# Folding a layer norm's gamma and beta into the next weight, and a new order of work, in a graph transformer on one NeuronCore

## The chip, the cores and the metric

The kernel is written in Bass, with every wait and signal placed by hand, and runs on one core of one Trainium2 chip. The metric is the device time of one execution in microseconds, as a median of several runs. The engines are TensorE (PE; PEld is its weight load), VectorE (DVE), ScalarE (ACT), GpSimd (POOL) and SyncE (SP), which issues all loads and stores from one queue. Each engine works through its own instructions in order; they meet only at semaphores.

## The reference, cut to what matters

Eight graphs of 1024 nodes with 256 features each. `h = relu(layernorm(x))` goes through three layers of the first network, the result is added to `x`, and the same is done with one attention layer (`_L1_gnn_ref`) whose output passes an ELU.

```python
for l in range(3):                                   # first network
    si = x @ attn_w[l, :d]
    sj = x @ attn_w[l, d:]
    scores = si[:, :, None] + sj[:, None, :] + attn_b[l]
    scores = jnp.where(scores >= 0, scores, 0.2 * scores)
    scores = jnp.where(mask, scores, -jnp.inf)
    attn = jax.nn.softmax(scores, axis=-1)
    agg = jnp.einsum('bij,bjd->bid', attn, x)
    h = layernorm(x + agg, g1[l], beta1[l])
    ff = jax.nn.gelu(h @ W1[l] + b1[l], approximate=False) @ W2[l] + b2[l]
    x = layernorm(h + ff, g2[l], beta2[l])
```

The attention layer is the same without bias and FFN: `Wh = h @ W`, scores from `Wh`, softmax over the neighbours, `elu(attention @ Wh)`. A row without neighbours gets the mean over all nodes.

## The kernel before

The 32 pairs of graph and layer are 32 steps in a hand-written `ORDER`: 24 FFN steps (layers 0 to 2) and 8 attention steps (layer 3; k = 6, 10, 14, 18, 22, 29, 30, 31), neighbours in the list belonging to different graphs. A graph's nodes are NT = 8 tiles of 128.

A step k first aggregates: `aggregate(k, t)` multiplies the unnormalised scores `pw` (f32, 1024 x 1024) by the node rows `xx`, 16 instructions for each tile t, into one of two PSUM banks OB. In an FFN step VectorE divides by the row sum, adds the residual into `xc` and takes statistics (`residual1`), GpSimd makes the reciprocal deviation (`ln_rstd`), ScalarE normalises, GpSimd multiplies by gamma and adds beta (`affine`, lines 541 and 543), TensorE transposes pairs of tiles into TH (`transpose_h`), and ScalarE and VectorE write the transposed rows as an f16 high half and an f16 low half (`hT`). Then come 16 passes n over the hidden features: `hidden(k, n)` makes 512 columns of the first product into bank FB (6 instructions), ScalarE does the GELU and writes its high half, VectorE (even n, line 1100) or GpSimd (odd n, line 554) the low half into `gT`, a ring of three, and `second(k, n)` adds the second product into OB (12 instructions). `hidden` runs LAG = 2 passes ahead. The bias b2 is the first product of each bank: `ones3` times `b2r`, four times a step. `residual2`, the second statistics and `affine` with the second gamma and beta end the step; GpSimd does the last four tiles of that (`tail`) at the head of the next step.

Between these pieces each step prepares the scores of step q = k + 1. VectorE sums the two score columns (`scores`, lines 1003 and 1008), splits them (`columns`), TensorE transposes them into TP (`transpose_c`, line 1498) and spreads them over RB (`spread_s1`, `spread_sj`), VectorE takes each row's masked maximum (`row_max`, line 1063), ScalarE writes the shifted mask `nms` (line 780), and then come 16 units: TensorE transposes half a tile row of the mask into one half of RB (`unit`), VectorE makes the scores from it (`score`, line 1086) and ScalarE exponentiates (line 765). A unit waits until the score two units earlier has left its half of RB. When each piece is due stands in tables by place: 0 to 7 are the aggregation tiles, 8 + n the passes, END the end of the step, -1 the place before tile 0. Which table a step uses depends on its `variant`: "early", "late", "very late", and "ahead" (q = 11, 15, 19, 23), where columns and maxima are already made two steps earlier.

In an attention step the aggregated rows go through `elu_a` and `elu_b` on VectorE and `final` on GpSimd. Eight steps (`GAT_AT`) also make the input of an attention step: x is loaded again (`x1_of`), added, normalised, transposed (line 1538), multiplied by the weight (`gat_product`) and summed (`gat_colsum`). Seven steps (`RAW_AT`) also load and normalise a new graph and convert its edges (line 1111).

The first layer's weights are split into f16 high and low halves at the start (`w0_low`), the others in steps 0 and 1 (`load_piece`, `piece_high`, `piece_low`), stored to DRAM, and loaded back at each change of layer.

TensorE's order in an FFN step before:

```python
for t in range(NT):
    aggregate(k, t)
    if t in (4, 6):
        transpose_h(k, t // 2 - 2)
    prepare(k, t)
...
for n in range(LAG):
    hidden(k, n)
...
transpose_h(k, 2)
```

## Time and profile before

| | |
|---|---|
| median of 3 runs | 2702.7 us (2700.8 to 2707.65) |
| profiled execution | 2699.2 us, span from first to last instruction 2697.5 us |
| TensorE busy | 2357.2 us, 87% |
| VectorE, ScalarE, GpSimd busy | 1833.0, 1566.6, 1286.5 us |
| mean granted TensorE clock | 0.957 |
| DMA | 128 MB, 48 GB/s over the span |

Spans are read against the profiled execution, which lies 3.5 us under the median. The steps are cut at the first aggregation product of each: step 0 begins at 57.4 us, step 2 at 247.9, step 5 at 504.6, step 10 at 968.7, step 14 at 1290.9, step 26 at 2270.0, step 29 at 2531.0, step 31 at 2662.7.

### The profile page before, as it was taken

The numbers are of one execution on the slowest core, as the hardware profiler recorded it, in microseconds if no ns is written. First come the engines' busy times: TensorE is split into PE (matmuls) and PEld (weight loads), VectorE is DVE, ScalarE is ACT, GpSimd is POOL, SyncE is SP. The second block draws the span as 40 slices with busy tenths as digits, with TensorE's granted clock in tenths as the row PEclk, the third lists the DMA queues.
The fourth block names the chain that finished last, engine by engine and source line by source line (L and its number), as shares of the span: only waits on it lengthen the run. The fifth ranks groups of instructions, "written<-read, shape, count | busy, mean of one in ns | idle before, by whom it ended". The sixth has DMA issues, their size and how long they took to land.

```text
span 2697.5 us, 41567 instructions
## 1 busy us (share of the span) xinstructions
PE 2357.2 (87%) x14721; PEld 1760.6 (65%) x14721; DVE 1833.0 (68%) x4906; ACT 1566.6 (58%) x2423; POOL 1286.5 (48%) x2212
## 2 busy tenths in 40 slices
PE   3889999878899989899798988999888999999868
PEld 2566666646676666676576766677665677667656
DVE  7677677437677667776677766868657576666655
ACT  4457666445566555565556665665636556656544
POOL 5555465523365434644356542655434555446411
PEclk9999999989899999999899998999989999999988
DMA  4312021101120112110211102111121010100000
GB/s 175 123 40 86 5 86 40 52 4 40 59 87 5 40 43 91 52 36 9 73 61 55 36 13 74 56 52 36 38 92 40 24 36 9 36 9 21 23 12 30
DMA packets 66051, 128.15 MB, mean 48 GB/s; under 512 B 12956, under 2 KB 53172, under 8 KB 62772
## 3 DMA queue, kind: packets, MB, share of 16 engines
q1 hardware_dynamic: 65844, 125.50, 14.0%
q8 instruction: 116, 1.90, 0.3%
q14 instruction: 91, 0.75, 0.1%
HBM read 110.80 MB, written 14.68 MB: 47 GB/s over the span
## 4 chain that ended last, share of the span: by engine, by line
PE 57%; DVE 21%; ACT 8%; POOL 6%; issue 6%; DMA 1%; SPq 0%; DVEq 0%; POOLq 0%; ACTq 0%
PE OB L1413 35%; PE FB L1413 13%; DVE mj L1063 5%; PE RB L1413 4%; DVE pw L1086 4%; ACT nms L780 3%; DVE junk L1003 2%; PE TH L1413 2%; DMA adjst<-in_x 1%; DVE st L952 1%; DVE junk L1008 1%; POOL xc L541 1%; DVE xc L979 1%; ACT xc L725 1%; ACT gT L759 1%
## 5 line engine op out<-in xcount | busy, mean ns | idle before, releaser
L1413 PE MATMUL OB<-xx,pw 128*128 128x257 f32 x4096 | 980.4, 398 | 26.0 <-DVE xc L979 16.7
L1413 PEld LDWEIGHTS OB<-xx,pw 128*128 128x128 f32 x4096 | 798.3, 199 | 168.7 <-DVE xc L979 21.1
L1413 PE MATMUL FB<-hT,wb 128*128 128x512 f16 x2304 | 564.1, 383 | 67.6 <-DVE gT L1100 42.0
L1413 PE MATMUL OB<-wb,gT 128*128 128x256 f16 x4608 | 575.2, 273 | 4.3 <-POOL gT L554 4.2
L1413 PEld LDWEIGHTS OB<-wb,gT 128*128 128x128 f16 x4608 | 449.8, 98 | 137.5 <-POOL gT L554 8.1
L554 POOL TENSOR_TENSOR gT<-g,gT 128x512 f16<-128x512 f32 x192 | 229.2, 1194 | 612.7 <-ACT gT L759 612.3
L725 ACT ACTIVATE xc<-xc,nb,rs 128x256 f32<-128x256 f32 x384 | 212.8, 589 | 375.3 <-POOL nb L529 375.2
L1086 DVE SCALAR_TENSOR_TENSOR pw<-r2s,sj,RB 128x512 f32<-128x512 f32 x512 | 365.4, 740 | 77.6 <-PE RB L1413 74.7
L1413 PEld LDWEIGHTS FB<-hT,wb 128*128 128x128 f16 x2304 | 212.9, 98 | 276.7 <-DVE gT L1100 49.1
L541 POOL TENSOR_TENSOR xc<-xc,gb 128x256 f32<-128x256 f32 x384 | 289.9, 755 | 94.0 <-ACT xc L725 94.0
L765 ACT ACTIVATE pw<-pw,sj 128x512 f32<-128x512 f32 x512 | 327.7, 708 | 8.6 <-DVE pw L1086 8.3
L1063 DVE CUSTOM_DVE_ANT_0 mj<-RB,nm 128x1024 bf16<-128x1024 f32 x256 | 303.3, 1215 | 3.7 <-issue 2.9
L1413 PE MATMUL RB<-identb,nms 128*128 128x128 bf16 x2048 | 207.2, 236 | 106.8 <-DVE pw L1086 82.5
L780 ACT ACTIVATE nms<-nm,cc 128x1024 bf16<-128x1024 bf16 x256 | 279.7, 1136 | 8.9 <-DVE cc L1078 8.9
L1100 DVE TENSOR_TENSOR gT<-FB,gT 128x512 f16<-128x512 f32 x192 | 132.2, 688 | 216.2 <-ACT gT L759 216.0
L1413 PEld LDWEIGHTS RB<-identb,nms 128*128 128x128 bf16 x2048 | 149.3, 104 | 154.8 <-DVE pw L1086 118.3
L754 ACT ACTIVATE FB<-FB,b1c 128x512 f32<-128x512 f32 x192 | 125.8, 655 | 163.2 <-PE FB L1413 162.9
L521 POOL TENSOR_SCALAR ve<-mv 128x2 f32<-128x2 f32 x256 | 58.2, 227 | 321.8 <-DVE mv L955 307.4
L962 DVE RECIPROCAL rden<-OB 128x1 f32<-128x1 f32 x192 | 31.8, 166 | 246.4 <-PE OB L1413 245.9
L754 ACT ACTIVATE g<-FB,b1c 128x512 f32<-128x512 f32 x192 | 130.9, 682 | 114.1 <-PE FB L1413 114.1
L526 POOL TENSOR_TENSOR rs<-ve,mhalf 128x2 f32<-128x2 f32 x256 | 180.0, 703 | 21.3
L1008 DVE CUSTOM_DVE_ANT_0 junk<-xx,aw 128x256 bf16<-128x256 f32 x256 | 165.4, 646 | 0.0
(112 smaller groups left out, 2565.6 us busy)
## 6 DMA issues: line engine op xcount, KB each, us to landing
wb<-w_scratch SPq DMA_DIRECT2D x19, 2048.0 KB, 7.8
adjst<-in_adj SPq DMA_DIRECT2D x56, 512.0 KB, 4.2
xx<-in_x SPq DMA_DIRECT2D x16, 512.0 KB, 5.5
nm<-in_L_gnn_W SPq DMA_DIRECT2D x6, 1024.0 KB, 9.4
gb<-in_L_gnn_g SPq DMA_DIRECT2D x48, 128.0 KB, 2.8
gb<-in_L_gnn_beta SPq DMA_DIRECT2D x48, 128.0 KB, 3.4
adjst<-in_x SPq DMA_DIRECT2D x6, 1024.0 KB, 6.8
out_x<-adjst SPq DMA_DIRECT2D x48, 128.0 KB, 1.7
```

Of the source, the lines that this page charges most:

```text
L526: pool.tensor_tensor(out=rs[:, kind, c], in0=ve[:, kind, c], in1=mhalf[:, :], op=ALU.pow)\
L541: pool.tensor_tensor(out=v, in0=v, in1=gb[:, 0, :], op=ALU.mult).then_inc(mul_done[kind], 1)
L554: pool.tensor_tensor(out=gT[:, i % GRING, 1, :], in0=g32[:, :], in1=gT[:, i % GRING, 0, :], op=ALU.subtract).then_inc(glo_odd, 1)
L725: act.activation(dst, src, ACT.Relu if kind in (LNR, LNG) else ACT.Identity, bias=nb[:, kind, t:t + 1], scale=rs[:, kind, t:t + 1])\
L754: act.activation(dst, src, ACT.Gelu, bias=b1c[:, layer(k), f:f + 1], scale=1.0 / W_SCALE)\
L765: act.activation(v, v, ACT.Exp, bias=sj2[:, q % 2, jt:jt + 1]).then_inc(exp_done, 1)
L780: act.activation(nms[:, it, :], nm[:, slot(q), it, :], ACT.Identity, bias=cc[:, it:it + 1])\
L1008: dve.tensor_tensor_reduce(out=junk[:, 1, :], in0=src, in1=aw[:, l, 1, :], scale=1.0, scalar=0.0, op0=ALU.mult, op1=ALU.add, accum_out=sc[ ...
L1063: dve.tensor_tensor_reduce(out=mj[:, n % 2, :], in0=RB[:, :], in1=nm[:, g % 3, t, :], scale=1.0, scalar=-3e38, op0=ALU.add, op1=ALU.max, a ...
L1086: dve.scalar_tensor_tensor(out=pw[:, jt, half], in0=r2s[:, half], scalar=sj8[:, q % 2, jt:jt + 1], in1=RB[:, (u % 2) * HALF:(u % 2 + 1) * ...
L1100: dve.tensor_tensor(out=gT[:, i % GRING, 1, :], in0=FB[i % 2][:, :], in1=gT[:, i % GRING, 0, :], op=ALU.subtract).then_inc(glo_even, 1)
L1413: return pe.matmul(o, lhsT, rhs, start=first, stop=last)
```

## The change

**Fold.** The first gamma multiplies the rows of W1 when it is split (`g1s`, times the scale of 64), and W1 times beta is added to b1 (`bias_product`, 16 one-column products for each layer, and `bias_sum`). The transposes then read rows that are only normalised. The residual still needs gamma and beta: GpSimd's `affine` waits for the transpose of its pair, and stands in the passes n = 1, 3, 9 and 11. It adds beta plus b2, a sum made once, stored in `bb_scratch` and loaded in beta's place; the four `ones3` products of each FFN step are gone.

**Order on TensorE.** `hidden(k, 0)` and `hidden(k, 1)` stand ahead of the last aggregation tile; the transposes follow tiles 3, 5 and 7 and pass 2.

**Preparation.** `transpose_c` moves behind tile 0, the spreads to tiles 1 to 3, and the maxima are spaced further apart. For the steps in `CARRY` (0, 1, 6, 7, 11, 15, 19, 23, 24, 30, 31) the last four units are left to that step's own tiles 0 and 1 (step 6: the last eight, tiles 0 to 2), and some units use TH and TP in place of RB. In attention steps a unit is scored and exponentiated in its own tile. Score sums ahead of steps 12, 16, 20 and 24 move into the attention steps' tiles 0 to 3. In step 5 the work for the attention input moves from the aggregation into the passes.

**Loads.** At the start the first layer's score weights come first; the rows of b1, g1 and beta1 come ahead of most of the edges; the other score weights come last. In a step the load of x for the attention input is issued before gamma and beta of the second normalisation. The selector `sel` is built from 8 columns and copied out by VectorE.

```diff
-MAX_FE = {2: (0,), 3: (1,), 4: (2,), 5: (3,), 6: (4, 5), 7: (6, 7)}
+CARRY = {0} | {k for k in range(1, STEPS) if is_gat(k - 1) or k in VERY_LATE}
+GAT_FFN_LATE = {5}
...
+MAX_FE = {2: (0,), 3: (1,), 4: (2,), 5: (3,), 6: (4,), 7: (5,), 8: (6,), 9: (7,)}
...
+MAX_FD = {3: (0, 1), 4: (2,), 5: (3, 4), 6: (5,), 7: (6, 7)}
...
+UNITS_FE = {11: (0, 1), 12: (2,), 13: (3,), 14: (4, 5), 15: (6,), 16: (7,), 17: (8,), 18: (9, 10), 19: (11,),
+            20: (12,), 21: (13, 14), 22: (15,)}
...
+UNITS_FC = {11: (0, 1), 12: (2, 3), 13: (4, 5), 14: (6, 7), 15: (8, 9), 16: (10, 11), 17: (12, 13, 14, 15)}
...
+        if k in CARRY:
+            return dict(col=None, ct=0, s1=1, sj=3, row=MAX_FD, units=UNITS_FE, shift=SHIFT_FE)
...
-            return dict(col=None, ct=-1, s1=0, sj=1, row=MAX_FE, units=UNITS_FC, shift=SHIFT_FC)
-        return dict(col=None, ct=-1, s1=0, sj=1, row=MAX_FE, units=UNITS_FE, shift=SHIFT_FE)
+            return dict(col=None, ct=0, s1=1, sj=2, row=MAX_FC, units=UNITS_FC, shift=SHIFT_FC)
+        return dict(col=None, ct=0, s1=1, sj=2, row=MAX_FE, units=UNITS_FE, shift=SHIFT_FE)
...
+def carried(k):
+
+    if k not in CARRY:
+        return {}
+    if k - 1 in GAT_FFN_LATE:
+        return {0: (8, 9, 10, 11), 1: (12, 13), 2: (14, 15)}
+    return {0: (12, 13), 1: (14, 15)}
+
+
+def score_bank(q, u):
+
+    if q in CARRY and u in (8, 9, 12, 13, 14, 15):
+        return ("TH", "TP")[u % 2]
+    return ("R0", "R1")[u % 2]
...
-                load_gb(gb1, g1, beta1, 0, gb1_ready)
                 load_gb(gb2, g2, beta2, 0, gb2_ready)
+                sp.wait_ge(bb_done, 1)
+                sp.dma_start(bb_scratch.rearrange("l d -> (l d)").unsqueeze(0), st1[0:1, 0:LAYERS * D])\
+                    .then_inc(bb_stored, 16)
+                sp.wait_ge(bb_stored, 16)
+                load_gb(gb1, g1, bb_scratch, 0, gb1_ready)
...
-                if l < LAYERS and k > 0:
-
-                    sp.wait_ge(aff_done[1], 8 * fi(k))
-                    load_gb(gb2, g2, beta2, l, gb2_ready)
                 if k in GAT_AT:
                     gg = GAT_AT[k]
                     if gg < 6:
...
                     sp.dma_start(x1_of(gg), x_v[gg]).then_inc(x1_ready, 16)
+                if l < LAYERS and k > 0:
+
+                    sp.wait_ge(aff_done[1], 8 * fi(k))
+                    load_gb(gb2, g2, beta2, l, gb2_ready)
...
                 for r in [32 * v + NT * part for v in range(2) for part in range(3)]:
-                    pool.affine_select(out=sel[:, :, :], in_=sel[:, :, :], compare_op=ALU.not_equal,
-                                       fill=1.0, base=-r, pattern=[[-1, NT], [0, P]],
+                    pool.wait_ge(const_ready, n)
+                    pool.affine_select(out=sel8[:, :], in_=sel8[:, :], compare_op=ALU.not_equal,
+                                       fill=1.0, base=-r, pattern=[[-1, NT]],
                                        channel_multiplier=1).then_inc(const_ready, 1)
...
-                pool.wait_ge(norm_done[kind], n)
+                if kind == LN1:
+                    pool.wait_ge(ht_done, 4 * fi(k) + t // 2 + 1)
+                else:
+                    pool.wait_ge(norm_done[kind], n)
...
+                    if n == 11:
+                        ln_rstd(LN2, i, 0)
+                    if n in (1, 3, 9, 11):
+                        j = (1, 3, 9, 11).index(n)
+                        affine(LN1, k, 2 * j)
+                        affine(LN1, k, 2 * j + 1)
...
+            act.wait_ge(g1s_done, 1)
+            act.wait_ge(w0_ready, 32)
+            for kd in range(KD):
+                c = slice(kd * FF, (kd + 1) * FF)
+                act.activation(wb[:, 0, c], nm2.bitcast(f32)[:, c], ACT.Identity, bias=zero1[:, 0:1],
+                               scale=g1s[:, 0, kd:kd + 1]).then_inc(w0_hi, 1)
+            act.activation(wb[:, 2, :], nm2.bitcast(f32)[:, 2048:4096], ACT.Copy, scale=W_SCALE).then_inc(w0_hi, 1)
...
             def gat_step(k):
                 gat = GAT_AT.get(k)
-                before(k)
                 for t in range(NT):
                     elu_a(k, t)
                     if t >= 1:
                         elu_b(k, t - 1)
                     prepare(k, t)
-                    unit_scores(k, t)
+                    for u in carried(k).get(t, ()):
+                        score(k, u)
+                    for u in prep_tables(k)["units"].get(t, ()):
+                        score(k + 1, u)
...
+            def bias_sum(l):
+
+                dve.wait_ge(bw_done, l + 1)
+                dve.tensor_tensor(out=b1c[:, l, :], in0=TPf[:, 0:FT], in1=b1c[:, l, :], op=ALU.add)\
+                   .then_inc(b1c_done, 1)

...
+            def bias_product(l):
+
+                if l == 0:
+                    pe.wait_ge(w0_ready, 32)
+                    pe.wait_ge(wc_done, 1)
+                else:
+                    pe.wait_ge(piece_ready, 16 * (2 * l - 1))
+                pe.wait_ge(*tp_after[-1])
+                raw = nm2[:, 0:4096].bitcast(f32)
+                for f in range(FT):
+                    for kd in range(KD):
+                        ins = mm(TPf[:, f:f + 1], raw[:, kd * FF + f * P:kd * FF + (f + 1) * P],
+                                 be1[:, l, kd:kd + 1], kd == 0, kd == KD - 1)
+                ins.then_inc(bw_done, 1)
+                tp_after.append((b1c_done, l + 1))
...
                     if f == 0:
                         u = bank_uses(k) + NT + 2 * h + b
                         pe.wait_ge(ob_free, u - 1)
-                        mm(OB[b][:, :].rearrange("p (c d) -> p c d", c=2), ones3[:, :],
-                           b2r[:, layer(k):layer(k) + 1, :].broadcast_to([P, 2, D]), True, False)
                     if b == 0:
                         pe.wait_ge(*glo(i))
                     w2h, w2l = wb[:, 2, f * D:(f + 1) * D], wb[:, 3, f * D:(f + 1) * D]
...
-                    pe.wait_ge(x_done, 16 * q + u - 1)
+                if b == "TH" and th_after:
+                    pe.wait_ge(*th_after[-1])
+                elif b == "TP":
+                    pe.wait_ge(*tp_after[-1])
+                elif u >= 2:
+                    pe.wait_ge(x_done, 16 * q + (u - 3 if q in CARRY and u in (10, 11) else u - 1))
                 for i in range(HT):
-                    c = (u % 2) * HALF + i * P
-                    ins = mm(RB[:, c:c + P], nms[:, HT * h + i, jt * P:(jt + 1) * P], identb[:, :], True, True)
+                    ins = mm(BANK[b][:, i * P:(i + 1) * P], nms[:, HT * h + i, jt * P:(jt + 1) * P],
+                             identb[:, :], True, True)
                 ins.then_inc(mt_done, 1)
+                if b == "TH":
+                    th_after.append((x_done, 16 * q + u + 1))
+                elif b == "TP":
+                    tp_after.append((x_done, 16 * q + u + 1))
...
                 gat = GAT_AT.get(k)
-                early = k + 1 not in VERY_LATE
-                prepare(k, -1)
+                early = gat is not None and k not in GAT_FFN_LATE
                 for t in range(NT):
+                    if t == NT - 1:
+                        hidden(k, 0)
+                        hidden(k, 1)
                     aggregate(k, t)
-                    if t in (4, 6):
-                        transpose_h(k, t // 2 - 2)
                     prepare(k, t)
-                    if gat is not None and not early:
...
+                    if t in (3, 5, 7):
+                        transpose_h(k, t // 2 - 1)
                 for n in range(NF):
                     prepare(k, 8 + n)
...
+                    if k in GAT_FFN_LATE:
+                        if n in (1, 2, 4, 5):
+                            gat_product(gat, (1, 2, 4, 5).index(n))
+                        if n in (0, 1, 2, 4):
+                            gat_transpose(gat, (0, 1, 2, 4).index(n))
+                    if n == (3 if k in GAT_FFN_LATE else 2):
                         transpose_h(k, 3)
```

## Rows read from the trace of the kernel before

**Rows 1.** The page, part 1: busy us (share of the span) xinstructions.

```profile
PE 2357.2 (87%) x14721; PEld 1760.6 (65%) x14721; DVE 1833.0 (68%) x4906; ACT 1566.6 (58%) x2423; POOL 1286.5 (48%) x2212
```

**Rows 2.** The view of the cores: span, mean granted clock.

```profile
core 0: 2697.5 us, clock 0.957
```

**Rows 3.** TensorE's groups by shape: busy us, mean ns | idle before, releasers.

```profile
L1413 PE MATMUL OB<-xx,pw 128*128 128x257 f32 x4096 | 980.4, 398 | 26.0 <-DVE xc L979 16.7 <-DVE hT L1156 9.3
...
L1413 PE MATMUL FB<-hT,wb 128*128 128x512 f16 x2304 | 564.1, 383 | 67.6 <-DVE gT L1100 42.0 <-issue 21.1 <-DVE hT L1094 4.4
L1413 PE MATMUL RB<-identb,nms 128*128 128x128 bf16 x2048 | 207.2, 236 | 106.8 <-DVE pw L1086 82.5 <-ACT nms L780 11.6 <-DVE M L1063 10.5
L1437 PE MATMUL TH<-ident,xc 128*128 128x128 f32 x384 | 59.2, 277 | 22.3 <-POOL xc L543 21.5 <-ACT xx L790 0.8
L1413 PE MATMUL TH<-gw,mj 128*128 128x256 f16 x384 | 51.8, 289 | 28.7 <-DVE mj L1136 20.1 <-DVE hT L1094 8.6
```

**Rows 4.** The view of waits: us in total, times, longest.

```profile
PE TP L1498 <- DVE c L1031: 47.5, 16, 29.2
```

**Rows 5.** Windows: start, k=0, 2, 5, 14; length, busy by engine, clock, DMA.

```profile
core 0: us, PE busy (x) PEld busy (x) DVE busy (x) ACT busy (x) POOL busy (x), PEclk, DMA share, GB/s
0.00:57.40 57.40, 11.87 (x82) 7.49 (x83) 43.63 (x104) 25.14 (x31) 33.96 (x60) 1.00 0.57 204
57.40:163.70 106.30, 86.87 (x521) 62.66 (x518) 76.37 (x184) 60.16 (x90) 55.30 (x90) 0.93 0.28 92
247.90:331.50 83.60, 79.56 (x518) 58.13 (x518) 55.48 (x147) 52.69 (x80) 43.67 (x73) 1.00 0.10 32
504.60:642.50 137.90, 100.70 (x599) 72.42 (x599) 69.29 (x201) 66.38 (x105) 56.54 (x106) 0.88 0.13 43
1290.90:1347.00 56.10, 43.35 (x194) 33.55 (x194) 35.40 (x105) 29.52 (x49) 14.73 (x24) 0.80 0.19 68
```

**Rows 6.** Windows of k=10, 14, 18, 22 alone: their sum and mean.

```profile
sum 208.20, PE 163.57 PEld 127.60 DVE 140.50 ACT 117.79 POOL 58.94; mean PE 40.89 PEld 31.90 DVE 35.12 ACT 29.45 POOL 14.74
```

**Rows 7.** Timeline of TensorE in k=2: start us, us, what.

```profile
286.88 0.38 PE L1413 MATMUL OB<-b2r,ones 128*128 128x512 bf16 x1
287.10 0.82 PE L1413 MATMUL OB<-wb,gT 128*128 128x256 f16 x6
...
294.81 1.46 PE L1413 MATMUL FB<-hT,wb 128*128 128x512 f16 x6
...
297.41 0.61 PE L1413 MATMUL RB<-identb,nms 128*128 128x128 bf16 x8
```

**Rows 8.** The groups of instructions: GpSimd's low half and its multiplication by gamma.

```profile
L541 POOL TENSOR_TENSOR xc<-xc,gb 128x256 f32<-128x256 f32 x384 | 289.9, 755 | 94.0 <-ACT xc L725 94.0
L554 POOL TENSOR_TENSOR gT<-g,gT 128x512 f16<-128x512 f32 x192 | 229.2, 1194 | 612.7 <-ACT gT L759 612.3
```

**Rows 9.** Timeline of ScalarE in k=26: in brackets the idle time before.

```profile
2284.70 1.09 ACT L725 ACTIVATE xc<-xc,nb,rs 128x256 f32<-128x256 f32 x2 [3.73 <-POOL nb L529]
```

**Rows 10.** Timeline of VectorE in k=10.

```profile
971.43 0.42 DVE L1008 CUSTOM_DVE_ANT_0 junk<-xx,aw 128x256 bf16<-128x256 f32 x1
...
972.47 1.22 DVE L1063 CUSTOM_DVE_ANT_0 mj<-RB,nm 128x1024 bf16<-128x1024 f32 x1
...
984.03 0.94 DVE L1008 CUSTOM_DVE_ANT_0 junk<-xx,aw 128x256 bf16<-128x256 f32 x1
...
995.82 1.40 DVE L1086 SCALAR_TENSOR_TENSOR pw<-r2s,sj,RB 128x512 f32<-128x512 f32 x2
```

**Rows 11.** Timeline of TensorE in k=10.

```profile
996.62 1.26 PE L1413 MATMUL RB<-identb,nms 128*128 128x128 bf16 x8 [3.31 <-DVE pw L1086]
```

**Rows 12.** The chain of waits in k=5: start us, us, what.

```profile
518.44 7.39 DMA adjst<-in_x
```

**Rows 13.** Timeline of TensorE in k=29.

```profile
2570.90 1.11 PE L1538 MATMUL TP<-ident,mj 128*128 128x128 f32 x4 [12.30 <-ACT mj L725]
```

**Rows 14.** Timeline of all engines at the start.

```profile
14.79 7.82 POOL L505 TENSOR_SCALAR_AFFINE_SELECT sel<-sel 64x1024 bf16<-64x1024 bf16 x6
...
28.92 2.95 DVE L1111 TENSOR_SCALAR nm<-pw 128x1024 bf16<-128x1024 int32 x4
```

529 lines of the change are left out of this document (271 added, 258 removed).

## The prediction

> **What bounds the kernel now.** The page comes first: TensorE is busy for 2357.2 us of the 2697.5 us span, VectorE for 1833.0, ScalarE for 1566.6, GpSimd for 1286.5 [rows 1]. So TensorE sets the time, and 340 us of its span are idle. The view of the cores adds a second loss: the mean granted clock is 0.957 [rows 2], and 4.3% of 2697.5 us is 116 us of clock not granted (where that falls into idle time it costs nothing).
>
> TensorE's groups by shape say what the idle time waits for [rows 3]: the mask products into RB waited 106.8 us, 82.5 of it for VectorE's score instruction at L1086; the first FFN product into FB 67.6 us, mostly for the low half of gT at L1100; the transposes of the normalised rows 22.3 us, 21.5 for GpSimd's affine at L543; the attention products into TH 28.7 us; the aggregation 26.0. The view of waits adds the c transposes, 47.5 us, of which the longest, 29.2, is the start [rows 4].
>
> The windows, cut where each step's aggregation begins, say where [rows 5]. An ordinary FFN step (k=2) takes 83.6 us with 79.6 busy. The exceptions are the start (57.4 us, 11.9 busy), k=0 (106.3, 86.9) and k=5 (137.9, 100.7, clock 0.88). The four attention steps k=10, 14, 18 and 22, each ahead of a step whose preparation was begun two steps early, take 208.2 us with 163.6 busy [rows 6]; k=14 runs at a clock of 0.80 [rows 5]. In all there are 24 FFN steps and 8 attention steps.
>
> **The change, part by part.**
>
> *Bias products removed.* Each FFN step issues four b2r products, and the next instruction follows one after 0.22 us (286.88 to 287.10) [rows 7]. 96 x 0.22 = 21 us on the engine that sets the time. They wait for VectorE to empty a bank; the first real product inherits that wait, so I count nothing for it. Bounds: 19 (some passes wait for another engine anyway) and 24 (at the half clock). Gain 21.
>
> *Transposes no longer wait for gamma and beta.* GpSimd does two instructions per tile, L541's at 0.755 us [rows 8] and another of the same shape, so a pair of tiles puts 3.0 us between normalisation and transpose. But the transposes also move one tile earlier (behind tiles 3 and 5 rather than 4 and 6), which takes a tile of about 3.5 us of cover away. At k=26, which begins at 2270.0, ScalarE starts the first pair at 2284.70, released by GpSimd, which is still in the tail of the step before when the first statistics come [rows 9]; it ends 15.8 us into the step, and the fourth tile ends at 14 to 15 us. So in ordinary steps this edit breaks even, and in k=0 and 23, where the next graph's statistics stand ahead of it, a stall stays. Gain 10 of 22.3, bounds 0 and 20.
>
> *Two FFN products before the last aggregation tile.* The GELU, its copy and the subtraction for products 0 and 1 now run under that tile, and the third product, which waits for them, finds them done. FB's 67.6 us are 2.8 a step. A little comes back, since the last pair's normalisation must fit in before product 4. Gain 42, bounds 20 and 60. If the cover is gone, because the second transposes come late, the stall stands ahead of product 0 and the gain is 20.
>
> *The affine moves into the FFN loop* (n = 1, 3, 9, 11). A pass is 2.6 us of TensorE (294.81 to 297.41) [rows 7], and GpSimd's subtraction, 1.19 us [rows 8], comes every second pass, so 5.2 us hold 1.19 + 3.0 = 4.2 us. In the eleven steps that also carry a next graph's or an attention input's work it is more: k=5 has 56.5 us of GpSimd against 43.7 in k=2 [rows 5], 12.9 in four portions of 3.2, and 4.2 + 3.2 is 7.4 in 5.2: 2.2 us late, of which half is hidden by the ring of three. Cost 10, bounds 0 and 40.
>
> *Mask products and scores.* Sixteen score instructions close a step's preparation; VectorE does two in 1.40 us [rows 10]. Four of the sixteen now go into the next step's first tiles in eleven steps, and TH and TP are two more banks between the engines. In attention steps a unit is scored in its own tile instead of one tile later; that is the 3.31 us wait at 996.62 and shorter ones behind it [rows 11], and of the 11 us idle in such a step I take 7. VectorE gets two tiles' score sums (four of 0.42 us, 1.7 in all) in each of those steps' first four tiles, beside its own work under 3.5 us: about level. Of the 96 us of RB waits behind the start: gain 50, bounds 20 and 75. The aggregation's 26.0 us are mostly waits at the head of attention steps behind VectorE's queue, which is shorter by two tiles of score sums and a mask row of 1.22 us [rows 10]: gain 12, bounds 0 and 20.
>
> *The c transpose* moves from before tile 0 to behind it. Of the 18.3 us inside steps: gain 12, bounds 5 and 16. The mask rows that follow later have passes of TensorE to hide under.
>
> *k=5, k=29 and the order of loads.* At k=5 GpSimd sat behind the load of x (7.39 us at 518.44) [rows 12] with the first pair's statistics queued behind it. That load is now issued before gamma and beta of the second normalisation, and the attention products go into the FFN loop. At k=29 a transpose held TensorE for 12.30 us [rows 13] with ready aggregation tiles queued behind it; it now stands one tile later. Of 28.7 + 12.3 us: gain 24, bounds 10 and 35. New is the end of k=5, where eight mask rows of 1.22 us [rows 10], 9.8 in all, fall in four passes of 2.6: cost 6, bounds 0 and 12.
>
> *The start.* The selector's six instructions took 7.82 us of GpSimd and now work on 8 columns; VectorE's four mask conversions, 2.95 us [rows 14], leave the place between the c transpose and its copy; and four of sixteen units leave the start at 0.7 us each. 2.6 + 2.8 less 0.4 for the new bias products: gain 5, bounds 0 and 8.
>
> *The clock.* Low clocks stand where the idle time is: 0.88 in k=5 and 0.80 in k=14 against 1.00 in k=2 [rows 5]. With half the idle time gone a bit less than half of the 116 us should return. Gain 50, bounds 20 and 90.
>
> Sum: 21 + 10 + 42 - 10 + 50 + 12 + 12 + 24 - 6 + 5 + 50 = 210 us. Laid over the steps that is: the four attention steps 58 (208 to 150), k=5 31 (138 to 107), k=0 and 23 together 22, the last attention steps and k=6 20, the start 5, and 3.5 in each of the 21 other FFN steps. Against the profiled execution's own 2699.2 us it makes 2489; the median of the runs shown is 3.5 us higher, so 2492.
>
> One row speaks against moving the affine: a score sum at L1008 takes 0.42 us in one place and 0.94 in another, where GpSimd is busy [rows 10]. The Trainium skill, "SBUF — State Buffer", section "Who interferes with whom", says that VectorE and GpSimd share one port pair as an exclusive lock, which VectorE instructions with both inputs in SBUF also take; by that rule, the trace agrees. Its consequence here is the second rival, priced from rows.
>
> **The rivals.**
>
> *VectorE stays in the way (18%).* Its work is moved, not less. If its queue in attention steps and at the end of k=5 sets the pace, the scores give 20, the clock 25, the aggregation 4, the attention terms 14: 73 less, 2565. For it: VectorE is busy 35 of the 52 us of such a step [rows 6]. Against: it has waits in their last tiles.
>
> *VectorE and GpSimd slow each other (8%).* In eleven steps four score sums fall beside the moved affines, each 0.52 us longer, and what follows waits: 11 x 2.1 = 23 us, 2515.
>
> *More falls away than I count (17%).* With TensorE fed all through, the clock gives 90 and the scores 65: 2437.
>
> *GpSimd becomes the bound, slower than before (4%).* If the four affine pairs stand wholly ahead of a subtraction that a product waits for, 24 x 4 x 3.0 = 288 us are added: 2780. It ends slower once some 73% of them is exposed. Against: GpSimd is busy 43.7 of 83.6 us in k=2 [rows 5], and the residual wants the affine only at n = 8.
>
> *Only the removed products count (3%):* every stall just moves, 2682.
>
> **How the numbers follow.** My forecast, 2492 us, has 50%, with a range of its own of 2460 to 2530. The range for 8 in 10 takes in the second rival, the third and most of the first: 2435 to 2580. A difference under 0.3% (8 us) can't be told from none. Faster by more has 0.95, the same 0.01, slower 0.04.
>
> **What would show it.** No b2r products; FB's waits under 30 us; the transposes waiting for ScalarE, not GpSimd; RB's waits under 60 us; the four attention steps at 36 to 40 us with a clock above 0.93; ordinary FFN steps at 80 to 81 us; k=5 near 107. It is wrong if products wait for gT of L554 for more than 30 us, if attention steps stay above 45 us, or if the mean clock stays at 0.96.

## The result, and the profile after

The changed kernel takes 2634.65 us (median of 4 runs, 2623.89 to 2639.5) against 2701.75 us before (4 runs, 2700.29 to 2707.65), a ratio of 0.9742 with a 95% interval of 0.9709 to 0.9776. The forecast was 2492, its range 2435 to 2580. The kernel is faster, as forecast, but by 67 us and not by 210. The profiled execution took 2635.33 us.

Part 1 of the page and the view of the cores, against [rows 1, 2]:

```profile
PE 2320.5 (88%) x14721; PEld 1733.9 (66%) x14721; DVE 1848.1 (70%) x4914; ACT 1579.8 (60%) x2426; POOL 1271.1 (48%) x2199
```

```profile
core 0: 2633.6 us, clock 0.973
```

TensorE is busy for 37 us less and idle for 313 us, where 340 were idle before; the granted clock rose from 0.957 to 0.973. TensorE's groups by shape, against [rows 3]:

```profile
L1484 PE MATMUL OB<-xx,pw 128*128 128x257 f32 x4096 | 960.0, 389 | 22.2 <-DVE xc L1025 13.1 <-DVE hT L1203 8.5 <-ACT pw L799 0.4
L1484 PE MATMUL OB<-wb,gT 128*128 128x256 f16 x4608 | 574.1, 275 | 27.6 <-DVE xc L1025 18.1 <-POOL gT L612 9.5
L1484 PE MATMUL FB<-hT,wb 128*128 128x512 f16 x2304 | 568.5, 385 | 73.9 <-DVE gT L1147 57.3 <-issue 11.4 <-ACT g L788 5.2
L1484 PE MATMUL RB<-identb,nms 128*128 128x128 bf16 x1784 | 164.9, 227 | 83.5 <-DVE pw L1133 65.3 <-ACT nms L816 14.2 <-DVE M L1109 3.5
L1525 PE MATMUL TH<-ident,xc 128*128 128x128 f32 x384 | 59.9, 280 | 24.3 <-ACT xc L757 24.3
L1484 PE MATMUL TH<-gw,mj 128*128 128x256 f16 x384 | 48.7, 278 | 19.6 <-DVE mj L1183 18.5 <-DVE hT L1141 1.2
```

FB's waits were to fall from 67.6 us to under 30 and are 73.9. RB's were to fall from 106.8 to under 60 and are 83.5. The transposes wait for ScalarE now, but as long as before. The c transpose's line in the view of waits was 47.5 us in 16 waits [rows 4]; now it is:

```profile
PE TP L1584 <- DVE c L1077: 11.8, 2, 11.1
```

Of these 11.8 us, 11.1 are the start. A wait of another kind is new: in k=30 a c transpose waits 3.5 us for a unit's score to leave TP.

The windows of the start, k=0, 2, 5 and 10, cut as in [rows 5], and the sum of the four attention steps alone, against [rows 6]:

```profile
core 0: us, PE busy (x) PEld busy (x) DVE busy (x) ACT busy (x) POOL busy (x), PEclk, DMA share, GB/s
0.00:44.70 44.70, 15.78 (x99) 13.39 (x99) 34.89 (x103) 21.68 (x25) 18.54 (x47) 1.00 0.75 271
44.70:159.50 114.80, 93.05 (x548) 68.17 (x546) 75.58 (x175) 58.80 (x88) 48.89 (x80) 0.88 0.25 85
254.80:336.80 82.00, 77.52 (x513) 58.09 (x513) 54.87 (x147) 50.82 (x77) 43.37 (x73) 1.00 0.09 33
510.30:620.00 109.70, 92.38 (x561) 67.17 (x562) 64.99 (x191) 59.15 (x96) 56.86 (x106) 0.92 0.16 54
948.10:982.60 34.50, 31.77 (x176) 26.64 (x177) 31.34 (x100) 29.46 (x49) 14.42 (x24) 1.00 0.21 80
```

```profile
sum 138.00, PE 127.07 PEld 106.54 DVE 125.38 ACT 117.83 POOL 57.71; mean PE 31.77 PEld 26.64 DVE 31.34 ACT 29.46 POOL 14.43
```

Cut by steps in this way, each step from its first aggregation product to the next one's, the two profiled executions are 63.9 us apart, and they divide like this (the last column is worked out from the same cut of a run told below):

| steps | before | changed | gain | predicted | three edits (E5) |
|---|---|---|---|---|---|
| start | 57.4 | 44.7 | 12.7 | 5 | 44.9 |
| attention, k=10, 14, 18, 22 | 208.1 | 138.0 | 70.1 | 58 | 138.0 |
| k=5 | 137.9 | 109.7 | 28.2 | 31 | 107.1 |
| k=6, 29, 30, 31 | 221.2 | 210.5 | 10.7 | 20 | 212.6 |
| k=0 and 23 | 205.8 | 218.9 | -13.1 | 22 | 203.4 |
| the 21 other FFN steps | 1867.0 | 1911.8 | -44.8 | 74 | 1849.7 |

The sum predicted is 210 us, the sum that came 63.9. The first four rows gave 122 us where 114 were forecast. All of the miss lies in the 23 FFN steps of the last two rows: 96 us predicted, 58 lost, a difference of 154. In the 21 ordinary ones TensorE's idle time rose from 110 to 160 us: FB's from 59 to 64, RB's from 13 to 46, OB's behind the second product from 9 (with the bias products) to 22, the attention products' from 1 to 9; of the larger groups only the c transpose's fell, from 18 to 1. By steps, 22.9 of the 44.8 us lie in k=7, 11, 15 and 19, which also prepare a new graph, 11.0 in k=1 and 10.1 in k=9, 13, 17 and 21; k=2, 4, 25, 26 and 27 are 0.9 to 1.5 us shorter each.

The timeline of k=26, which begins at 2209.7, shows the first of the causes, at the end of the aggregation (the number in brackets is the idle time of the engine before):

```profile
2240.08 0.60 ACT L793 ACTIVATE gT<-FB 128x512 f16<-128x512 f32 x1
2240.48 3.64 PE L1484 MATMUL OB<-xx,pw 128*128 128x257 f32 x16
...
2244.15 0.17 DVE L1008 RECIPROCAL rden<-OB 128x1 f32<-128x1 f32 x1 [3.04 <-PE OB L1484]
...
2245.43 0.66 DVE L1147 TENSOR_TENSOR gT<-FB,gT 128x512 f16<-128x512 f32 x1
...
2246.15 1.47 PE L1484 MATMUL FB<-hT,wb 128*128 128x512 f16 x6 [1.60 <-DVE gT L1147]
...
2246.92 0.20 POOL L584 TENSOR_TENSOR nb<-ng,rs 128x2 f32<-128x2 f32 x1
2247.07 1.16 POOL L612 TENSOR_TENSOR gT<-g,gT 128x512 f16<-128x512 f32 x1
2247.15 1.09 ACT L757 ACTIVATE xc<-xc,nb,rs 128x256 f32<-128x256 f32 x2 [1.96 <-POOL nb L584]
...
2248.14 0.64 ACT L788 ACTIVATE FB<-FB,wc 128x512 f32<-128x512 f32 x1
```

The GELU of product 0 is through, with its copy, at 2240.68, under the last aggregation tile, as the prediction wanted. But its low half on VectorE starts at 2245.43: it stands behind the residual of tile 7, and VectorE sits idle for 3.04 us until that tile is summed. GpSimd's low half of product 1 stands behind the reciprocal deviation of tile 7's pair (nb, 2246.92), and ScalarE's gelu of product 2 behind that pair's normalisation (2247.15). Three in-order queues hold the chain until tile 7 is done, and the two products now ahead of that tile push it back by 2.5 us: it ends 34.4 us into the step, and 31.9 in the run below that has them behind it (E4).

The timeline of k=11, which begins at 982.6, shows the second cause:

```profile
1022.24 1.15 POOL L612 TENSOR_TENSOR gT<-g,gT 128x512 f16<-128x512 f32 x1
...
1022.63 2.45 DVE L1158 TENSOR_SCALAR nm<-adjst 128x1024 bf16<-128x1024 int32 x2
...
1023.35 1.17 POOL L599 TENSOR_TENSOR xc<-xc,gb 128x256 f32<-128x256 f32 x1
...
1024.60 1.05 POOL L601 TENSOR_TENSOR xc<-xc,gb 128x256 f32<-128x256 f32 x1
...
1026.42 0.73 POOL L601 TENSOR_TENSOR xc<-xc,gb 128x256 f32<-128x256 f32 x1
...
1027.69 0.69 DVE L1158 TENSOR_SCALAR nm<-adjst 128x1024 bf16<-128x1024 int32 x1 [0.48 <-DMA adjst<-in_adj]
1027.78 1.17 POOL L581 TENSOR_TENSOR rs<-ve,mhalf 128x2 f32<-128x2 f32 x1
...
1029.25 1.09 ACT L757 ACTIVATE xx<-xx,nb,rs 128x256 f32<-128x256 f32 x2 [2.60 <-POOL nb L584]
1029.42 0.69 DVE L1158 TENSOR_SCALAR nm<-adjst 128x1024 bf16<-128x1024 int32 x1 [1.03 <-DMA adjst<-in_adj]
...
1030.25 0.67 ACT L788 ACTIVATE g<-FB,wc 128x512 f32<-128x512 f32 x1
...
1030.97 1.04 PE L1484 MATMUL FB<-hT,wb 128*128 128x512 f16 x4 [0.78 <-ACT g L788]
```

The moved affine pair (four instructions, 1023.35 to 1027.15) stands ahead of the next graph's reciprocal deviation, whose nb releases ScalarE only at 1029.25; ScalarE had sat idle for 2.60 us with the gelu of product 3 queued behind, and TensorE waits for that gelu. The prediction had GpSimd late at its own subtraction; it is late at four small instructions for which ScalarE waits.

A third difference stands in k=0 and k=1, and the prediction's sum has nothing for it: there the new bias products (16 of them for a layer, 32 instructions in the trace) hold TensorE for 5.3 and 4.9 us (from 119.88 and from 218.46 on).

### The profile page after: what moved, and what is told of

It reads as the page before. It is cut to its first block, busy times and chain, and to the rows that moved or that the text cites. A ratio compares the mean times of both kernels' runs of the same rounds, so it can differ in the third digit from the quotient of the medians.

```text
span 2633.6 us, 41679 instructions
## 1 busy us (share of the span) xinstructions
PE 2320.5 (88%) x14721; PEld 1733.9 (66%) x14721; DVE 1848.1 (70%) x4914; ACT 1579.8 (60%) x2426; POOL 1271.1 (48%) x2199
## 3 DMA queue, kind: packets, MB, share of 16 engines
q8 instruction: 117, 1.92, 0.3%
## 4 chain that ended last, share of the span: by engine, by line
PE 55%; DVE 24%; issue 8%; ACT 8%; POOL 6%; DMA 1%; DVEq 0%; SPq 0%; POOLq 0%; ACTq 0%
PE OB L1484 36%; PE FB L1484 12%; DVE pw L1133 5%; DVE mj L1109 3%; PE RB L1484 3%; ACT nms L816 3%; DVE junk L1049 3%; DVE st L998 2%; PE TH L1484 2%; DVE gT L1147 2%; DVE xc L1025 1%; DVE junk L1054 1%; ACT gT L793 1%; POOL rs L581 1%; PE TH L1525 1%
## 5 line engine op out<-in xcount | busy, mean ns | idle before, releaser
L1484 PE MATMUL OB<-xx,pw 128*128 128x257 f32 x4096 | 960.0, 389 | 22.2 <-DVE xc L1025 13.1
L1484 PEld LDWEIGHTS OB<-xx,pw 128*128 128x128 f32 x4096 | 771.4, 193 | 163.4 <-DVE xc L1025 19.6
L1484 PE MATMUL FB<-hT,wb 128*128 128x512 f16 x2304 | 568.5, 385 | 73.9 <-DVE gT L1147 57.3
L799 ACT ACTIVATE pw<-pw,sj 128x512 f32<-128x512 f32 x512 | 334.0, 711 | 57.5 <-DVE pw L1133 57.0
L757 ACT ACTIVATE xc<-xc,nb,rs 128x256 f32<-128x256 f32 x384 | 212.6, 590 | 234.0 <-POOL nb L584 233.9
L1133 DVE SCALAR_TENSOR_TENSOR pw<-r2s,sj,RB 128x512 f32<-128x512 f32 x446 | 315.7, 738 | 43.7 <-PE RB L1484 43.0
L1484 PE MATMUL RB<-identb,nms 128*128 128x128 bf16 x1784 | 164.9, 227 | 83.5 <-DVE pw L1133 65.3
L788 ACT ACTIVATE FB<-FB,wc 128x512 f32<-128x512 f32 x192 | 125.7, 655 | 162.9 <-PE FB L1484 162.6
L1008 DVE RECIPROCAL rden<-OB 128x1 f32<-128x1 f32 x192 | 31.9, 166 | 256.0 <-PE OB L1484 255.4
L788 ACT ACTIVATE g<-FB,wc 128x512 f32<-128x512 f32 x192 | 130.7, 681 | 125.9 <-PE FB L1484 125.8
L1484 PEld LDWEIGHTS RB<-identb,nms 128*128 128x128 bf16 x1784 | 124.2, 101 | 115.3 <-DVE pw L1133 88.8
## 6 DMA issues: line engine op xcount, KB each, us to landing
adjst<-in_x SPq DMA_DIRECT2D x6, 1024.0 KB, 11.1
```

Of the source, the lines that this page charges most:

```text
L757: act.activation(dst, src, ACT.Relu if kind in (LNR, LNG) else ACT.Identity, bias=nb[:, kind, t:t + 1], scale=rs[:, kind, t:t + 1])\
L788: act.activation(dst, src, ACT.Gelu, bias=b1c[:, layer(k), f:f + 1], scale=1.0 / W_SCALE)\
L799: act.activation(v, v, ACT.Exp, bias=sj2[:, q % 2, jt:jt + 1]).then_inc(exp_done, 1)
L1133: dve.scalar_tensor_tensor(out=pw[:, jt, half], in0=r2s[:, half], scalar=sj8[:, q % 2, jt:jt + 1], in1=b, op0=ALU.max, op1=ALU.add).then_i ...
L1484: return pe.matmul(o, lhsT, rhs, start=first, stop=last)
```

## The experiments

Every run is compared with the kernel before on the same chip. "By the steps" means by the same cut of the profiled execution as in the table above. Where a difference to the changed kernel or between two runs is given, it is that of the two ratios times 2702 us; the ratios are each known to some 0.0015 to 0.003, so such a difference is good to 5 to 10 us, and where it is smaller the steps of the profiled executions carry the reading.

**E1, VectorE's first low half ahead of the last residual.**

```diff
                     if t == 7:
                         prepare(k, 7)
+                        if k not in GAT_FFN_LATE:
+                            g_low(k, 0)
                     residual1(k, t)
...
-                    if n % 2 == 0:
+                    if n % 2 == 0 and (n > 0 or k in GAT_FFN_LATE):
                         g_low(k, n)
```

> The changed kernel, in which VectorE makes the low half of the first gelu output (gT, L1147) ahead of the last residual of the aggregation instead of behind it (not in k=5). Theory A, the low half is late because it stands in VectorE's order behind a residual that waits for aggregation tile 7, while the 67 us of FB waits were predicted to fall to 30 and rose to 74: the wait of 1.60 us in front of hidden product 2 is gone in some 23 steps, FB waits fall from 74 to about 40 us, the time by 30 to 38 us to about 2600 (ratio to the kernel before 0.960 to 0.964). Rival, the wait only moves to the next consumer of VectorE's work (the low half of hT, the mask rows, the OB banks): FB falls but RB, OB or hT waits rise by as much, and the time stays within 8 us of 2634 (ratio 0.972 to 0.977).

Measured 2645.2 us, ratio 0.9775 (0.976 to 0.9789): not faster at all. FB's waits fall from 73.9 to 62.8 us and the time does not follow. In k=26, which begins at 2221.0 here, the wait of 1.60 us is gone, and one of 2.17 stands where one of 1.31 stood, a pair of passes later:

```profile
2257.43 0.69 POOL L581 TENSOR_TENSOR rs<-ve,mhalf 128x2 f32<-128x2 f32 x1
...
2258.20 0.20 POOL L584 TENSOR_TENSOR nb<-ng,rs 128x2 f32<-128x2 f32 x1
...
2258.35 1.16 POOL L612 TENSOR_TENSOR gT<-g,gT 128x512 f16<-128x512 f32 x1
...
2259.43 0.64 ACT L788 ACTIVATE FB<-FB,wc 128x512 f32<-128x512 f32 x1
...
2262.07 1.22 DVE L1109 CUSTOM_DVE_ANT_0 mj<-RB,nm 128x1024 bf16<-128x1024 f32 x1
...
2263.21 0.68 DVE L1147 TENSOR_TENSOR gT<-FB,gT 128x512 f16<-128x512 f32 x1
...
2263.95 1.47 PE L1486 MATMUL FB<-hT,wb 128*128 128x512 f16 x6 [2.17 <-DVE gT L1147]
```

The 21 ordinary steps take 1911.7 us, to a tenth what they took; k=0 and 23 take 10 us more. Theory A, VectorE's order alone, falls. GpSimd and ScalarE hold the same chain behind the same tile: product 2 is through at 2257.13, and its GELU starts at 2259.43, behind tile 7's normalisation. Its low half is then late once more, on VectorE, where mask rows, the last at 2262.07, stand ahead of it.

**E4, the two products behind the last tile again.**

```diff
                 for t in range(NT):
-                    if t == NT - 1:
-                        hidden(k, 0)
-                        hidden(k, 1)
                     aggregate(k, t)
...
+                hidden(k, 0)
+                hidden(k, 1)
                 for n in range(NF):
```

> The changed kernel with the first two hidden products behind aggregation tile 7 again, all else as changed. The prediction counted 42 us for having them ahead. Theory A, in-order VectorE takes nearly all of this back since its low half still follows the last residual: the time rises by under 12 us (ratio to the kernel before 0.973 to 0.979). Rival, the 42 us were gained and something else lost them: the time rises by 30 to 50 us (ratio 0.985 to 0.993).

Measured 2616.43 us, ratio 0.967 (0.9655 to 0.9684): 19 us faster than with the products ahead. Neither theory had this. By the steps, the 21 ordinary ones fall by 22.0 us and k=5 by 2.5, and k=0 and 23 rise by 3.9. FB's group in this run:

```profile
L1484 PE MATMUL FB<-hT,wb 128*128 128x512 f16 x2304 | 569.7, 386 | 46.0 <-DVE gT L1147 40.0 <-ACT g L788 5.1
```

Against the changed kernel's 73.9 us, the 11.4 of "issue" are gone (product 0, waiting 0.5 to 1.05 us ahead of tile 7 in steps such as k=11 at 1013.06, after VectorE made the low half of hT at 1012.27), and 17 of the wait for low halves: products 0 and 1 stand between tile 7 and product 2 again, as cover. The prediction's gain of 42 us is a loss of about 19.

**E9 and E11, nothing of the gelu chain behind tile 7** (not in k=5; the transposes of pair 3 move one pass later with it). E9 keeps the products ahead; E11 has them behind. Both have the edits of E2 and E3, below. The first hunk, VectorE's, is in E9 alone.

```diff
+                        if k not in (0, 5, 23):
+                            g_low(k, 0)
                     residual1(k, t)
...
-                ln_rstd(LN1, i, 3)
+                if k in GAT_FFN_LATE:
+                    ln_rstd(LN1, i, 3)
...
                     if n % 2 == 1:
                         g_low(k, n)
+                    if n == 1 and k not in GAT_FFN_LATE:
+                        ln_rstd(LN1, i, 3)
...
                     if n == 1:
                         ht_high(k, 2)
+                    if n == (1 if k in GAT_FFN_LATE else 2):
                         normalise_pair(LN1, k, 3)
```

> The changed kernel (first two hidden products ahead of aggregation tile 7), in which nothing of the gelu chain stands behind tile 7's statistics any more: VectorE's first low half ahead of the last residual, GpSimd's reciprocal deviation of LN1 pair 3 behind its low half of product 1, ScalarE's normalisation of that pair behind gelu 2 and TensorE's transposes of it one pass later; with the two edits that do not touch this (reciprocal deviations first at n=1 and 3; the transposes of k=0 and k=23 later, no product ahead there). Without the un-anchoring these would stand near 2588. Theory of the anchor, each of the three in-order engines holds the chain until tile 7 is summed, and a product ahead only pushes tile 7 back: now the products ahead pay, FB waits on VectorE's low halves fall to 20 to 30 us and the time to 2545 to 2568 (ratio 0.941 to 0.949), at or under the same kernel with the products behind. Rival, it is TensorE's cover that is missing (two products fewer between tile 7 and hidden product 2) whatever the order elsewhere: above 2575 (ratio over 0.952).

> The kernel of three edits (products behind tile 7) with the same un-anchoring of GpSimd, ScalarE and TensorE, without VectorE's, which has its first low half behind the last residual anyhow. Theory of the anchor: with the products behind tile 7, its statistics are there by the time that product 1 is through gelu, so the order hardly matters: within 8 us of the kernel of three edits (ratio 0.942 to 0.948). Rival, the waits of 0.8 and 1.1 us in front of hidden products 2 and 4 come from the normalisation that ScalarE makes ahead of gelu 2: they go, 10 to 30 us less (ratio 0.934 to 0.941).

E9 measured 2561.17 us, ratio 0.9489 (0.9469 to 0.9509), E11 2562.57 us, ratio 0.9486 (0.9472 to 0.9501). The 2588 that E9 is held against was reckoned (E3 less E2's part), not run, but the ordinary steps have a run to be held against: they take 1875.3 us in E3 and 1849.0 in E9, 26 less. So freeing the chain is worth 26 us with the products ahead, and the anchor is real. The waits for VectorE's low halves fell less than expected, from 57.3 in the changed kernel to 39.2 us. With the products behind, freeing the chain is worth nothing (E11 is 10 us above E5, below, and 5.7 by the ordinary steps, about the 8 that were allowed for). The freed kernel with products ahead is no better than the kernels with products behind (1849.0 us in the ordinary steps, 1849.7 in E5), so in none of these runs did they pay: with all three queues freed, they break even.

**E3, the reciprocal deviations ahead of the moved affine.**

```diff
+                    first = early and n in (1, 3)
+                    if first and raw is not None:
+                        ln_rstd(LNR, raw, n // 2)
+                    if first and gat is not None:
+                        ln_rstd(LNG, gat, n // 2)
                     if n in (1, 3, 9, 11):
...
                         affine(LN1, k, 2 * j)
...
-                        if n in (1, 3, 5, 7):
+                        if n in (5, 7):
                             ln_rstd(LNR, raw, n // 2)
...
-                    if gat is not None and early and n in (1, 3, 5, 7):
+                    if gat is not None and early and n in (5, 7):
                         ln_rstd(LNG, gat, n // 2)
```

> The changed kernel, in which GpSimd makes the reciprocal deviations of the raw or graph-attention tiles at n=1 and n=3 ahead of the two LN1 affine pairs that the change moved there, instead of behind them (13 steps that are early and have such tiles). Theory B, the moved affine pairs (two times about 4 us) hold ScalarE's normalisation and the gelu behind it: the ScalarE waits of 2.1 to 2.6 us at these places, and the FB, OB and RB waits behind them, go; 2 to 3 us in each of 11 to 13 steps, 20 to 35 us in all, to about 2607 (ratio 0.961 to 0.968). Rival, these waits are covered by TensorE's products in hand and only their tail counts: under 8 us (ratio 0.972 to 0.976).

Measured 2598.01 us, ratio 0.9599 (0.9583 to 0.9616): 39 us faster than the changed kernel, a little more than expected, for the order of eight small instructions in each of 11 steps (not 13: k=0 and 23 are not "early"). Ten of the 11 are 2.8 to 4.5 us shorter; k=3 is not. In k=11 ScalarE goes from one to the next without a wait:

```profile
1013.62 1.92 DVE L1163 TENSOR_SCALAR nm<-adjst 128x1024 bf16<-128x1024 int32 x2
...
1014.48 0.51 POOL L576 TENSOR_SCALAR ve<-mv 128x2 f32<-128x2 f32 x1
...
1016.45 0.20 POOL L584 TENSOR_TENSOR nb<-ng,rs 128x2 f32<-128x2 f32 x1
...
1017.55 1.08 ACT L762 ACTIVATE xx<-xx,nb,rs 128x256 f32<-128x256 f32 x2
...
1018.53 0.67 ACT L793 ACTIVATE g<-FB,wc 128x512 f32<-128x512 f32 x1
```

The 21 ordinary steps fall from 1911.8 to 1875.3 us, RB's waits in them from 46 to 31 (that VectorE's scores were late because the low halves were is my reading, and was not run alone).

**E12, half of the first affine left out.** The multiplication by gamma on GpSimd is gone; the residual lacks it, the FFN products do not.

```diff
-                pool.tensor_tensor(out=v, in0=v, in1=gb[:, 0, :], op=ALU.mult).then_inc(mul_done[kind], 1)
-                pool.wait_ge(mul_done[kind], n)
+                if kind != LN1:
+                    pool.tensor_tensor(out=v, in0=v, in1=gb[:, 0, :], op=ALU.mult).then_inc(mul_done[kind], 1)
+                    pool.wait_ge(mul_done[kind], n)
```

> The changed kernel with the multiplication by gamma left out of the first normalisation's affine on GpSimd (the products see the normalised values as before; the residual stream lacks gamma, so the output is another), which takes 184 instructions of 0.72 to 1.17 us off GpSimd, half of the moved work. If the moved affine's length on GpSimd is what costs, as the reordering that won 37 us says: 15 to 30 us less (ratio 0.963 to 0.969). Rival, only the order counts and not the length: under 8 us (ratio 0.971 to 0.976).

Measured 2596.41 us, ratio 0.9611 (0.9594 to 0.9627), 35 us faster, above what either theory said (the left-out instructions are 192, not 184). Half of the length buys about as much as the right order: taking it out gives 35 us, where the prediction had 10 for the cost of all of it, with a bound of 40. Not all of the 35 need be GpSimd's queue. With these instructions gone VectorE's score sums take 303.7 us in place of 315.7, so some of it may be VectorE working undisturbed, and this run does not part the two. What the same cut would give in the kernel before was not run.

**E2, the transposes of k=0 and k=23 later.**

```diff
-                    if t == NT - 1:
+                    if t == NT - 1 and k not in (0, 23):
                         hidden(k, 0)
                         hidden(k, 1)
...
-                    if t in (3, 5, 7):
-                        transpose_h(k, t // 2 - 1)
+                    if k in (0, 23):
+                        if t in (4, 6):
+                            transpose_h(k, t // 2 - 2)
+                    elif t in (3, 5, 7):
+                        transpose_h(k, t // 2 - 1)
...
+                if k in (0, 23):
+                    hidden(k, 0)
+                    hidden(k, 1)
+                    transpose_h(k, 2)
```

> The changed kernel, in which the first three transpose pairs of steps k=0 and k=23 stand behind tiles 4, 6 and 7 of the aggregation, as in the kernel before, with the first two hidden products behind tile 7; the other steps as changed. Theory C, in these two steps GpSimd takes the raw statistics of tile 2j ahead of the LN1 pair j-1, so a transpose one tile earlier holds back the aggregation tile that its own successor needs: TH waits in the two steps fall from 12.7 and 11.1 us to under 4 each, and the time by 12 to 20 us to about 2618 (ratio 0.966 to 0.970). Rival, the chain through LN1 pairs is there at any place of the transposes (it is VectorE's edges of the same stretch that makes it long): the waits move to the FB and nms products, and the time stays within 5 us (ratio 0.973 to 0.976).

Measured 2624.43 us, ratio 0.9698 (0.9682 to 0.9714), 12 us faster. The two steps fall from 218.9 to 203.2 us and no other step moves by more than 2. The edit moves the first two products as well, but E4 moved these alone, and the two steps rose to 222.8; so the place of the transposes is worth 20 us there. The transposes' waits fall only in part, from 23.8 to 14.4 us in the two steps, where under 8 were expected. With the transpose one tile earlier, aggregation tile 2j stands behind it, the next graph's statistics of pair j behind tile 2j, and the LN1 pair j-1 behind these: theory C holds, at the low end of its price, and the chain that is left is the rival's part.

**E14 and E13, the tables of the mask work as before.** In 14 FFN steps from k=7 on, and in k=4, which uses the same tables, the passes in which mask rows, shifted masks and mask products are made; E14 on the changed kernel, E13 on E5, below.

```diff
-MAX_FE = {2: (0,), 3: (1,), 4: (2,), 5: (3,), 6: (4,), 7: (5,), 8: (6,), 9: (7,)}
+MAX_FE = {2: (0,), 3: (1,), 4: (2,), 5: (3,), 6: (4, 5), 7: (6, 7)}
...
-UNITS_FC = {11: (0, 1), 12: (2, 3), 13: (4, 5), 14: (6, 7), 15: (8, 9), 16: (10, 11), 17: (12, 13, 14, 15)}
+UNITS_FC = {9 + i: (2 * i, 2 * i + 1) for i in range(8)}
```

(MAX_FC, UNITS_FE, SHIFT_FE and SHIFT_FC are put back likewise.)

> The changed kernel with only the tables of the mask work put back as before in the same 14 steps. Theory of the tables: 8 to 30 us under the changed kernel (ratio 0.963 to 0.972), as the prediction's term for mask products and scores outside attention steps had the wrong sign. Rival, with the first two products ahead of the last tile the crowded tiles 6 and 7 hold the low half of hT for product 0 longer: 0 to 20 us more than the changed kernel (ratio 0.974 to 0.982).

> The kernel of three edits, with the hand-written tables of the mask work (which pass makes mask rows, shifted masks and mask units) as in the kernel before, in 14 FFN steps from k=7 on: units of the coming step from pass 1 on instead of pass 3. In the 21 ordinary FFN steps the waits of the mask products rose from 13.1 us (before) to 46.1 (changed) and stand at 33.9 in the kernel of three edits. Theory of the tables, the rest of the rise is the later start and the pairs of units in one pass: RB waits in these steps fall under 20 us and the time by 8 to 25 us (ratio 0.936 to 0.942). Rival, VectorE is crowded by the later affines and statistics at either place: RB, FB and OB waits together stay and the time is within 5 us or higher (ratio 0.943 or more).

E14 measured 2603.54 us, ratio 0.9618 (0.9602 to 0.9633), 33 us faster than the changed kernel and somewhat more than expected; E13 2547.12 us, ratio 0.941 (0.9393 to 0.9427), 11 us faster than E5. RB's group in E14:

```profile
L1483 PE MATMUL RB<-identb,nms 128*128 128x128 bf16 x1784 | 166.6, 226 | 54.1 <-DVE pw L1132 35.5 <-ACT nms L815 14.2 <-DVE M L1108 3.8
```

RB's waits are 54.1 us, under the 60 that the prediction wanted, and those of the 21 ordinary steps fall from 46 to 16. The retimed tables of the change made the waits that the prediction had the change remove.

**E5, three edits together** (E2, E3, and E4 in the other steps).

> The changed kernel with three of its placements altered together: reciprocal deviations ahead of the moved affine pairs at n=1 and n=3, the first two hidden products behind aggregation tile 7 in every step, and the transposes of k=0 and k=23 behind tiles 4, 6 and after those products. Alone, the first measured 37 us, the second 18 and the third 10 (2 of which lie in the same steps as the second). If the three costs lie in different places of a step: 60 us under the changed kernel, about 2572 (2565 to 2582, ratio 0.949 to 0.954). Rival, they share stalls (the gelu chain carries a late start into the next one), and a part is counted twice: 2585 to 2600 (ratio 0.955 to 0.961).

Measured 2555.83 us, ratio 0.9449 (0.9431 to 0.9467): 79 us faster than the changed kernel, more than either expectation and above the sum of its parts (39 + 19 + 12 = 70; the expectation's 37, 18 and 10 are the differences of the medians). The ratios can't tell 79 from 70. The steps can: E4's loss of 3.9 us in k=0 and 23 falls away beside E2's edit, and the ordinary steps fall by 62.1 us where E3 and E4 alone gave 36.5 and 22.0. So the three lie in different places, and no stall is counted twice.

**E8 and E10, a unit scored in the pass that issues it.** E8 in all FFN steps, E10 in k=1, 9, 13, 17 and 21, both on E5.

```diff
-                for u in prep_tables(k)["units"].get(at - 1, ()):
+                for u in prep_tables(k)["units"].get(at, ()) if at < END else ():
```

> The kernel of three edits, in which VectorE also scores a unit of the coming step in the pass in which TensorE issues it, not one pass later (FFN steps). If the waits of the mask products for a bank (65 us on VectorE's scores in the changed kernel, 2.47 and 0.85 us in a step such as k=9) come from that delay: 20 to 45 us less than the kernel of three edits (ratio to the kernel before 0.934 to 0.945 if that one stands at 0.952). Rival, VectorE then sits waiting for TensorE's unit ahead of its low halves, which come later: the mask waits fall and the FB and OB waits rise by as much or more, the time is within 10 us of the kernel of three edits or above it.

> The kernel of three edits, with a unit of the coming step scored in the pass in which TensorE issues it, in steps k=1, 9, 13, 17 and 21 alone, which make no tiles of another graph. In all steps this cost 59 us, most of it in the five steps that also hold graph-attention tiles (10 to 14 us each), while these five were 1.4 to 4 us shorter. If steps are independent: 8 to 14 us under the kernel of three edits, near 2545 (ratio 0.939 to 0.942). Rival, the gain came from the neighbouring steps' changed ends: within 4 us of it (ratio 0.943 to 0.947).

E8 measured 2614.52 us, ratio 0.9667 (0.9638 to 0.9695), 59 us slower than E5: RB's waits in the ordinary steps fall from 34 to 3 us, but those of the attention products rise from 1 to 40 and of the aggregation from 7 to 17. Its rival holds. E10 measured 2547.11 us, ratio 0.9429 (0.9415 to 0.9444), 5 us below E5 and between its two expectations. The ratios don't tell the two kernels apart; by the steps, the five are 10.7 us shorter together (k=1 by 3.5, k=9 by 0.2), and k=3 is 1.4 longer.

**E15, the last two affine pairs at n=7 and 9**, on E10 (`if n in (1, 3, 7, 9)` in place of `(1, 3, 9, 11)`).

> The kernel of three edits with five same-pass steps (2547 us), in which GpSimd makes LN1's last two affine pairs at n=7 and 9 instead of n=9 and 11, where an OB wait of 2.6 us for GpSimd's low half stands at the end of a step such as k=11 (OB waits in ordinary FFN steps are 32 us). If the crowd at the end of the pass makes it: 5 to 15 us less (ratio 0.937 to 0.941). Rival, the crowd only moves to n=7, where the raw and attention tiles' reciprocal deviations are: within 4 us or higher (ratio 0.942 or more).

Measured 2550.83 us, ratio 0.9422 (0.9408 to 0.9437): no gain, as the rival had it. By the steps, k=7, 11, 15 and 19 are 2.2 to 3.0 us longer, and k=8, 12, 16 and 20 up to 2.2 shorter.

**E6, attention steps scored one tile later.**

```diff
-                    for u in prep_tables(k)["units"].get(t, ()):
+                    for u in prep_tables(k)["units"].get(t - 1, ()):
                         score(k + 1, u)
...
                 elu_b(k, NT - 1)
+                for u in prep_tables(k)["units"].get(7, ()):
+                    score(k + 1, u)
```

> The changed kernel, in which VectorE scores the units of an attention step one tile later, as the kernel before did; the last four units stay in the step that follows. The four attention steps fell from 208 to 138 us. If the order on VectorE made this: the waits of the nms products of 3.3 and 2.1 us are back, each attention step is 6 to 12 us longer, the time 25 to 48 us up (ratio 0.983 to 0.992). Rival, it was the four units carried into the next step's two free banks that made it: each step is under 3 us longer, the time under 12 us up (ratio 0.974 to 0.979).

Measured 2671.52 us, ratio 0.9881 (0.9854 to 0.9909), 38 us slower than the changed kernel, as expected of VectorE's order. Three waits of 2.1 us are back in k=10; the one of 3.31 [rows 11] is not:

```profile
962.01 0.40 PE L1486 MATMUL RB<-identb,nms 128*128 128x128 bf16 x4 [2.10 <-DVE pw L1133]
```

The four steps take 178.5 us against 138.0 and, before, 208.1. The order on VectorE is thus 40 of the 70 us; the other 30 are the rest of what the change does there, the four units left to the next step among it, which was not run alone.

**E7, the kernel before without the b2r products** (its output lacks b2; `mm(o, gh, w2h, f == 0 and c == 0, False)` opens the bank).

> The kernel before with the 96 products that add the second bias left out (its output lacks b2), all else as it was. The prediction counted 21 us for them from their row (0.22 us each). If TensorE's time counts in full: 16 to 26 us under the kernel before (ratio 0.990 to 0.994). Rival, part of them stood in waits for the output bank that stay: under 10 us (ratio 0.996 to 1.000).

Measured 2686.25 us, ratio 0.993 (0.9907 to 0.9953), 19 us faster. By the steps it is less: the 24 FFN steps, which held the products, are 10.0 us shorter; the four attention steps, which held none, are 5.8 shorter, 5.1 of it in k=14 alone. A part comes back as waits: the second products waited 4.3 us and the bias products 9.5, the second products alone now wait 16.5, and FB's and RB's waits are 3 us longer each.

## Why the prediction was wrong, step by step

The step that failed is the overlap counted for two FFN products ahead of the last aggregation tile: 42 us forecast, and a loss of 19 measured (E4). Two more terms failed in the same FFN steps, the cost of the moved affine and the mask work outside the attention steps. The terms in their order:

- **Bias products, 21:** near; E7 measured 19 (13 to 25 by its interval), 10 by the FFN steps alone. The new bias products were counted as 0.4 us at the start and as nothing in k=0 and k=1, where they hold TensorE for 10.2 us.
- **Transposes, 10 of 22.3:** wrong in sign as a whole; they wait 24.3 us. In k=5, where the load of x moved as well, waits of 11.4 us are gone. In k=0 and 23 they rose from 9.5 to 23.8, and E2 against E4 puts the earlier place at 20 us there. The prediction saw that "a stall stays" there; it did not ask whether the tile now queued behind the transpose feeds the transpose after it.
- **Two FFN products before the last tile, 42:** the step that failed. That "the third product, which waits for them, finds them done" holds for ScalarE's work on them alone. The low half of product 0 stands behind the residual of tile 7 on VectorE, that of product 1 behind tile 7's deviation on GpSimd, gelu 2 behind its normalisation on ScalarE. E4 measured it at -19, outside its bounds of 20 and 60. The stall ahead of product 0 that I allowed for ("because the second transposes come late") came as well, at 11 us, and was not the main part.
- **The affine in the loop, cost 10:** mis-sized. It was costed against GpSimd's own subtraction (4.2 us in 5.2), as if that were all that waits. What waits first is ScalarE, for the deviations queued behind it: 39 us by the order alone (E3), 35 by half of the length (E12). The two overlap, and no run took the whole affine out of the loop, so whether the upper bound of 40 held is not shown.
- **Mask products and scores, 50:** two different things in one term. In the four attention steps RB's waits fell from 40 to 7 us, and E6 shows the mechanism named there; it was sized at 7 us a step, and putting VectorE's order back costs 10. Outside, in the ordinary steps, they rose from 13 to 46; E14 and E3 show 33 us for the tables and 39 for the affine (the two overlap in RB's waits: with E5's three edits in, the tables are worth 11). The prediction took a total of 96 us of waits and did not lay it over the steps: only 13 of it lay in ordinary FFN steps, so there was little to win and work was moved later for it.
- **Aggregation, 12:** mis-sized, 4 (26.0 to 22.2).
- **The c transpose, 12:** near, 14. Inside the steps its waits for the columns fell from 18.3 to 0.7 us, and the new one in k=30 is 3.5.
- **k=5, k=29 and loads, 24, and the end of k=5, -6:** right in time: k=5 took 109.7 where 107 was forecast, k=29 gave 9 of its 84.8. GpSimd's waits for the load of x, 21.8 us before, are gone. But the transposes of the attention input (TP<-ident,mj), 14.0 us before, wait 17.2 now, 8.4 of it still in k=29. No run took these parts apart.
- **The start, 5:** under-sized, 12.7. The first mask row starts at 27.3 us where it started at 35.5; no run took the start apart.
- **The clock, 50:** the loss within the steps fell from 117 to 72 us, which is 45, but most of it is in the attention steps and k=5. What it gave back in time was not measured by itself: clock that is not granted in idle time costs nothing. The row that shows it best is the aggregation's, 20.4 us less busy time (398 to 389 ns a product).

None of the rivals is what came. By its number the result lies past the first, "VectorE stays in the way" (2565), and nearest to "only the removed products count" (2682), but the attention steps and k=5 gave 98 us, so not every stall just moved. The first rival is nearest in kind, as VectorE's queue does hold the chain, but not in its place: in the attention steps and at the end of k=5 that queue did what was wanted. The second rival, VectorE and GpSimd slowing each other, had score sums longer by 0.52 us each: they take 315.7 us in all where they took 314.0, so there it did not come true. But three small instructions ahead of the shifted masks (L1119, L1121 and L1124) take 57.1 us in all where they took 38.6; whether that cost time, no run shows. None of the three signs of being wrong that the prediction named came up either (products wait 9.5 us for GpSimd's gT, the attention steps take 34.5 us, the clock is 0.973). Only its targets for FB's and RB's waits, missed by 44 and 24 us, told of the failure.

What stays open: 21 ordinary steps with three edits still take 1849.7 us, where the forecast had 1793. E13 takes 9 more off. In k=13 of E5 a wait of 2.47 us before a mask product remains, and in k=0 and 23 14.4 us of waits of the transposes. The bias products of the start, k=0 and k=1 (17.2 us of busy time for all) were not taken away in a run; k=1 is 8 us longer than before even with three edits.

The fastest versions are E13 and E10 at 2547 us, 5.8% under the kernel before and 3.3% under the changed one. E13:

```profile
PE 2297.1 (90%) x14721; PEld 1736.5 (68%) x14721; DVE 1841.8 (72%) x4914; ACT 1582.8 (62%) x2426; POOL 1276.6 (50%) x2199
```

## What to carry to other kernels

An instruction moved ahead of a wait is worth what its whole chain gains, so follow the chain through every in-order queue and ask what stands in front of each of its instructions; here one late tile stood in front of three of them. Where work is moved within a queue, cost it by what is queued behind it and who waits for that, down to the 0.2 us instructions, and not by whether the queue as a whole has room. And lay a total of waits over the steps before counting on a share of it: of RB's 107 us, 64 lay in the eight attention steps and 13 in the 21 ordinary FFN steps in which most of the retiming was made.

## What the runs showed of the hardware

GpSimd and VectorE slowed each other where both worked on SBUF. In k=11 of the changed kernel two mask conversions on VectorE take 2.45 us, beside GpSimd's multiplication of 1.17 us and addition of 1.05. Elsewhere in the same step a conversion takes 0.69 us (1029.42), an addition 0.73 (1026.42) and a multiplication 0.72 (at 1025.62). So VectorE's two took 1.07 us more in all, and GpSimd's two 0.77. In E3 the two conversions took 1.92 us beside small instructions of GpSimd, of which one then took 0.51 us in place of 0.19. It isn't always both: the conversion at 1027.69 keeps its 0.69 us, and GpSimd's instruction beside it, 0.69 elsewhere (2257.43 in E1), takes 1.17.

The Trainium skill, "SBUF — State Buffer", section "Who interferes with whom", calls the ports that the two share an exclusive lock. The pair at 1027.69, in which the one that started first kept its length, agrees with it; which of them waited for which in the first stretch can't be read from the rows. What the slowing costs in this kernel was not taken apart. Against the kernel before, the score sums take 1.7 us more.
